# Two transformer blocks on one core: each engine's order made by a planner with other lengths and other priorities

## The reference

```python
mod = (_silu(L0_c) @ L0_wmod).reshape(L0_c.shape[0], 6, 1, -1)
sa, ca, ga, sb, cb, gb = (mod[:, 0], ..., mod[:, 5])
h = _layernorm(x) * (1 + ca) + sa
x = x + ga * _L0_attn_ref(h, ...)     # linear attention, 16 heads, features elu(q)+1 and elu(k)+1
h = _layernorm(x) * (1 + cb) + sb
x = x + gb * _L0_ffn_ref(h, ...)      # layernorm, 8 experts 128->512->128 with gelu, the two best per token
...                                   # mod of block 1
h = _layernorm(x) * (1 + ca) + sa
x = x + ga * _L1_attn_ref(h, ...)     # layernorm, softmax attention, 8 heads of 16, values of 128 summed over the heads
h = _layernorm(x) * (1 + cb) + sb
x = x + gb * _L1_ffn_ref(h, ...)      # h plus the best of 8 experts 128->128
```

## Time and profile before

| | before |
|---|---|
| median of 3 runs | 711.38 us |
| lowest and highest | 710.27 and 713.83 us |
| span of the profiled execution | 708.6 us |
| PE busy | 619.4 us (87%) |
| DVE busy | 511.1 us (72%) |
| ACT busy | 385.6 us (54%) |
| POOL busy | 334.4 us (47%) |
| matmuls of line 1507 (fill) | 165 |
| mean granted clock of TensorE | 0.951 |
| moved by DMA | 106.4 MB, mean 150 GB/s |

### The profile page before, as it was taken

How to read it: one execution, slowest core, us unless ns; L and a number is a source line. 1 busy time by engine, 2 the same in 40 slices (tenths; PEclk the granted TensorE clock), 3 DMA queues, 4 the chain that set the end, 5 groups by cost and what they waited for, 6 DMA issues and landing times. The chain is left out here.

```text
span 708.6 us, 12005 instructions
## 1 busy us (share of the span) xinstructions
PE 619.4 (87%) x3832; PEld 395.1 (56%) x3832; DVE 511.1 (72%) x1298; ACT 385.6 (54%) x861; POOL 334.4 (47%) x363
## 2 busy tenths in 40 slices
PE   8996887998899979979998799968798899789974
PEld 4665556997899779958654633212233344344332
DVE  5576959447458966155887389999888665958997
ACT  2342134678967557635699377737274456366410
POOL 5112287065478577767034153754214137106934
PEclk9998999999999989999999899979898899999998
DMA  8200325588678869999944615450501616421221
GB/s 339 91 1 1 107 103 179 174 280 286 212 258 274 284 216 332 296 295 302 291 151 104 163 45 105 119 107 28 89 1 45 134 52 128 125 91 53 53 59 30
DMA packets 47421, 106.40 MB, mean 150 GB/s; under 512 B 7440, under 2 KB 22608, under 8 KB 45824
## 3 DMA queue, kind: packets, MB, share of 16 engines
q1 hardware_dynamic: 41808, 94.82, 44.9%
q0 software_dynamic: 5120, 10.50, 5.1%
q10 hardware_dynamic: 432, 0.34, 0.2%
HBM read 80.26 MB, written 25.17 MB: 149 GB/s over the span
## 5 line engine op out<-in xcount | busy, mean ns | idle before, releaser
L1359 DVE TENSOR_REDUCE mxs<-PS 128x2 f32<-128x1024 f32 x128 | 152.2, 1221 | 60.0 <-PE PS L1687 59.5
L1027 ACT ACTIVATE bufa<-PS 128x512 f32<-128x512 f32 x256 | 134.8, 608 | 63.5 <-PE PS L1713 32.1
L986 ACT ACTIVATE bufb<-PS,bufb 128x128 f32<-128x128 f32 x368 | 103.6, 376 | 69.5 <-PE PS L1652 68.4
L1652 PE MATMUL PS<-bufb 128*128 128x128 f32 x736 | 101.2, 285 | 12.6 <-DMA bufb<-in_experts_dram 10.2
L1652 PEld LDWEIGHTS PS<-bufb 128*128 128x128 f32 x736 | 93.3, 199 | 20.7 <-issue 16.3
L1660 PE MATMUL PS<-bufb 128*128 128x128 f32 x736 | 101.2, 284 | 3.0 <-ACT bufb L986 3.0
L1660 PEld LDWEIGHTS PS<-bufb 128*128 128x128 f32 x736 | 93.8, 199 | 7.2 <-ACT bufb L986 4.1
L842 POOL DMA_INDIRECT slots_in<-bufb x64 | 65.1, 1017 | 63.8 <-DVE bufb L1305 45.4
L1703 PE MATMUL PS<-stk 108*128 108x512 bf16 x256 | 87.0, 400 | 6.5 <-ACT bufa L1027 3.6
L1687 PE MATMUL PS<-stk 96*128 96x512 bf16 x256 | 80.9, 408 | 8.2 <-DVE mxs L1359 6.2
L853 POOL DMA_INDIRECT bufb<-slots_out,bufb x64 | 62.1, 971 | 50.9 <-issue 43.8
(11 more groups left out here) (302 smaller groups left out, 1031.6 us busy)
## 6 DMA issues: line engine op xcount, KB each, us to landing
bufb<-in_experts_dram SPq DMA_DIRECT2D x92, 514.0 KB, 5.2
slots_out<-bufb SPq DMA_DIRECT2D x30, 256.0 KB, 4.5
stk<-split SPq DMA_DIRECT2D x56, 128.0 KB, 7.6
bufb<-slots_in SPq DMA_DIRECT2D x25, 256.0 KB, 3.3
split<-terms SPq DMA_DIRECT2D x8, 768.0 KB, 3.8
slots_in<-hb SPq DMA_DIRECT2D x2, 1536.0 KB, 9.0
stk<-split SPq DMA_DIRECT2D x8, 384.0 KB, 4.6
X<-in_x_dram SPq DMA_DIRECT2D x4, 512.0 KB, 6.5
```

Source lines behind the costliest of these rows:

```text
L986: last = nc.scalar.activation(hs[:, n % HR, fc, :], ps[:, P * fc:P * fc + P], ACT.Gelu_apprx_tanh, bias=ws[:, n % WR, F + fc:F + fc + 1])
L1027: nc.scalar.activation(probs[:, i % PR, j, :], psum("s2", i, j), ACT.Exp, scale=DH1 ** -0.5)\
L1359: nc.vector.tensor_reduce(mxs[:, gr % 2, 2 * j:2 * j + 2, h], psum("s1", i, j).rearrange("p (c n) -> p c n", c=2), axis=AX.X, op=ALU.max)\
L1652: last = nc.tensor.matmul(ps[:, P * fc:P * fc + P], ws[:, n % WR, P * fc:P * fc + P], xq[:, q % 2, P * x:P * x + P], start=True, stop=True)
```

## The change

The planner's tables and the rules of `arrange` are exchanged; the steps, what each emits, and the buffers stay. Every row of every engine's list is computed anew.

- `LENGTH` gives way to two tables: `BUSY`, how long a step holds its engine, and `SEEN`, after what time its result is seen by others.
- Lags of transfers come from `LANDS` (from the end of the issue to the landing) and `SERVED`: transfers of SP and POOL go through one queue in the plan, each for its time. `HOP` depends on the engine that waits.
- `URGENCY` by kind gives way to `PRIORITY` by engine, kind and pair (`part`), numbers between -2300 and 1981, often larger than the rank itself.
- `NEAR` is 0.2 instead of 0.
- A step that takes PSUM banks may only be placed when what the freeing step waits for has been placed.
- PE's steps take twice their time for `WARM` = 4.0 us after a planned wait of over `COOL` = 3.0 us; ACT's steps whose function stands in another table come 1.3 us later.

Lengths of landings are single numbers; no landing is planned late.

```diff
-LENGTH = {
-    ('PE', 'pc'): 1.84, ('DVE', 'pc'): 0.44, ('PE', 'pm'): 2.0, ('ACT', 'pm'): 1.01, ('PE', 'pr'): 1.0,
...
-LATENCY = {
-    ('SP', 'bxl', 'PE', 'bxt'): 4.5, ('SP', 'cst', 'PE', 's1'): 8.5,
-}
-HOP = 0.1
-URGENCY = {
-    'akx': -10, 'an2': 160, 'anm': 10, 'aq': 10, 'bn2': 80, 'btr': -10, 'byo': 80, 'ckp': 40, 'cn4': -80, 'cpt': 20,
...
-NEAR = 0
+BUSY = {
+    ('ACT', 'akv'): 1.57, ('ACT', 'aot'): 0.96, ('ACT', 'aq'): 2.06, ('ACT', 'atr'): 1.81, ('ACT', 'bgt'): 0.26, ('ACT', 'bh'): 1.02,
...
+LANDS = {
+    ('POOL', 'bga'): 2.8, ('POOL', 'bsc'): 2.9, ('POOL', 'rga'): 3.4, ('POOL', 'rsc'): 4.8, ('SP', 'bw'): 2.95,
+    ('SP', 'bxl'): 2.5, ('SP', 'byo'): 1.75, ('SP', 'ckp'): 4.0, ('SP', 'cst'): 7.3, ('SP', 'cto'): 3.35,
...
+SERVED = {
+    'bga': 1.0, 'bsc': 1.0, 'bw': 1.6, 'bxl': 0.85, 'byo': 0.85, 'ckp': 1.0, 'cst': 3.4, 'cto': 2.3,
...
+PRIORITY = {
+    ('ACT', 'akv'): (-1622, -426, -375, 1032), ('ACT', 'aot'): (-498, -755, 388, 1401), ('ACT', 'aq'): (-361, -581, 1256, -1203), ('ACT', 'atr'): (439, 1767, -40, 717),
...
+TABLE = {"blg": 1, "ex": 1, "aq": 1, "akv": 1, "bh": 2}
+TABLE_LOAD, COOL, WARM = 1.3, 3.0, 4.0
+NEAR = 0.2
...
     for k in reversed(line):
-        rank[k] = ops[k][0] + max([lag + rank[u] for u, lag in users[k]], default=0.0)
+        rank[k] = ops[k][0] + max([0.0] + [lag + rank[u] for u, lag in users[k]])
     for k in ops:
-        rank[k] += URGENCY.get(k[1], 0.0)
+        rank[k] += PRIORITY[k[:2]][part(k)]
...
-        clock[k[0]] = t + length
+        idle[k] = t - clock[e]
+        if e == "PE":
+            if idle[k] > COOL:
+                slow = t + WARM
+            if t < slow:
+                busy, seen = 2 * busy, seen + busy
+        elif e == "ACT":
+            table = TABLE.get(k[1], table)
+        clock[e], end = t + busy, t + seen
+        if SERVED.get(k[1]) and e in ("SP", "POOL"):
+            end = max(queue, end)
+            queue = end + SERVED[k[1]]
```

More of the change, by code:

```diff
@@ new lines @@
+SEEN = {
+    ('ACT', 'aot'): 1.07, ('ACT', 'atr'): 1.93, ('ACT', 'bh'): 1.14, ('ACT', 'btr'): 1.45, ('ACT', 'by'): 0.5, ('ACT', 'cpq'): 1.27,
+    ('ACT', 'ctr'): 1.45, ('ACT', 'dtr'): 1.07, ('ACT', 'ex'): 0.59, ('ACT', 'pm'): 1.01, ('ACT', 'pvo'): 0.58, ('DVE', 'an1'): 2.48,
+    ('DVE', 'an2'): 2.14, ('DVE', 'anm'): 1.72, ('DVE', 'apr'): 2.48, ('DVE', 'bcm'): 1.13, ('DVE', 'bgb'): 1.21, ('DVE', 'bgt'): 0.61,
+    ('DVE', 'blg'): 4.4, ('DVE', 'bn1'): 2.48, ('DVE', 'bn3'): 2.49, ('DVE', 'brk'): 4.14, ('DVE', 'cn1'): 1.64, ('DVE', 'cn3'): 1.64,
+    ('DVE', 'cn4'): 2.14, ('DVE', 'cpq'): 1.4, ('DVE', 'dl2'): 1.1, ('DVE', 'dn1'): 1.63, ('DVE', 'dw'): 2.92, ('DVE', 'dx'): 1.21,
+    ('DVE', 'dy'): 2.55, ('DVE', 'en1'): 1.69, ('DVE', 'fin'): 1.27, ('DVE', 'msp'): 0.79, ('DVE', 'mx'): 1.22, ('DVE', 'pvw'): 2.33,
+    ('DVE', 'rds'): 2.57, ('PE', 'akv'): 1.89, ('PE', 'akx'): 2.32, ('PE', 'anm'): 1.14, ('PE', 'aot'): 1.04, ('PE', 'apr'): 1.95,
[5 rows of a table added]
+}
@@ L329, in arrange @@
 def arrange(ops, start):
-    users, left, est, rank = {k: [] for k in ops}, {}, {}, {}
-    for k, (_, deps, _, _) in ops.items():
+    users, left, est, rank, giver = {k: [] for k in ops}, {}, {}, {}, {}
+    for k, (_, _, deps, _, give) in ops.items():
         left[k], est[k] = len(deps), 0.0
@@ L335, in arrange @@
             users[d].append((k, lag))
+        if give:
+            giver[("PE",) + give] = k
+    line, n = [], dict(left)
     todo = [k for k in ops if not left[k]]
-    line, n = [], dict(left)
     while todo:
@@ L361, in arrange @@
                 t = max(clock[e], est[k])
-                if ops[k][2]:
-                    t = max(t, min(vacant[ops[k][2]]))
+                if ops[k][3]:
+                    if any(d not in done for d in before_take[k]):
+                        continue
+                    t = max(t, min(vacant[ops[k][3]]))
+                if e == "ACT" and TABLE.get(k[1], table) != table:
+                    t += TABLE_LOAD
                 if t < 1e8:
@@ L366, in arrange @@
             if when:
-                k = min((k for k in when if when[k] <= min(when.values()) + NEAR), key=lambda k: (-rank[k], when[k]))
+                near = min(when.values()) + NEAR
+                k = min((k for k in when if when[k] <= near), key=lambda k: (-rank[k], when[k]))
                 if first is None or (when[k], -rank[k]) < first[:2]:
@@ L370, in arrange @@
         t, _, k = first
-        length, _, take, give = ops[k]
+        busy, seen, _, take, give = ops[k]
+        e = k[0]
         if take:
@@ L375, in arrange @@
             vacant[take][n], count[take][n] = 1e9, count[take][n] + 1
-        idle[k] = t - clock[k[0]]
-        clock[k[0]] = t + length
+        idle[k] = t - clock[e]
[10 more added lines that the diff above has]
+            queue = end + SERVED[k[1]]
         if give:
             cls, n, _ = use[give]
-            vacant[cls][n] = t + length
-        order[k[0]].append(k[1:])
-        ready[k[0]].remove(k)
+            vacant[cls][n] = end + HOP["PE"]
+        order[e].append(k[1:])
+        ready[e].remove(k)
+        done.add(k)
         for u, lag in users[k]:
-            est[u], left[u] = max(est[u], t + length + lag), left[u] - 1
+            est[u], left[u] = max(est[u], end + lag), left[u] - 1
             if not left[u]:
```

93 lines of the change are left out of this document (65 added, 28 removed), and 22 rows, old and new, of tables (BUSY, PRIORITY, SEEN).

## The result

The kernel after takes 716.0 us in the median of 20 runs (711.3 to 722.6), the kernel before on the same chip 712.6: a ratio of **1.006** with a 95% interval of 1.0035 to 1.0086. The forecast was 697 us. Runs more than 1.5% above the fastest of their kernel have no part in any ratio here, one of the kernel before at 2056 us among them. The change is slower by 0.6%, about the least that a measurement can tell, and 19 us above the forecast. The profiled execution spans 713.2 us; the sum that gave -14.0 us is judged against this: it is +4.6 us.

The account below looks back on a forecast made before the run. PE's order was taken to bound the kernel from 110 to 680 us, DVE's at the end. Terms summed to -14.0 us, so 694.6 + 2.8 gave 697 us, own range 686 to 706, 674 to 719 with rivals.

Parts of the forecast that it names:

- Opening: Up to the first experts: they start 6.4 us later, but earlier PE work and a vanished token wait give -4.0 us.
- Table loads: ACT switches between gelu and exp less often, 17 loads for 23, mostly in idle time: -2 us.
- Weights behind the stacks: Expert weights issued behind attention stacks: waits of 4 us (pair 2, tile 17) and 2.4 (pair 3, tile 9); -3 us.
- pair 3's experts: Pair 3's experts move behind the first attention, so score steps start after less PE work: -3 us.
- Gate of the stacks: Attention batches 4, 5 and 7: less PE work covers a stack's issue and landing, so PE waits more: +3 us.
- Last experts: Score steps now stand between the last experts' steps, so their 5.0 us of weight waits go: -5 us.
- End: From the last maxima on, DVE's list holds the same steps: nothing gained or lost.
- Collisions: Rival: three more DVE and POOL steps blocking each other cost 16 us and eat the gain, 711 to 713; chance 0.16.
- Late landings: Rival: stacks landing late at three short gates make PE wait and lower its clock, 719 us; chance 0.20.
- The plan holds: Rival: two fifths of PE's idle and low-clock time go rather than a sixth, 675 us; chance 0.19.
- three signs: Forecast wrong if first experts start after 119 us, attention's clock stays at 0.92 or falls, or a gate wait exceeds 5 us.
- the middle's -3: Between opening and last experts: weights behind the stacks -3, pair 3's experts -3, gate of the stacks +3 us.

Follow-up runs that it names:

- f3: Kernel after with the load of the stacks' fixed rows (ckp) and the turning of pair 3's tokens (btr) moved later; 0.9988 of before.
- f2: Kernel after with only pk, POOL's building of the stacks' constant patterns, moved later, ahead of the first gather; 1.0002 of before.
- e3: Kernel after with the end of the order of before, from a planned 595 us on; 0.9985 of before.
- g1: Kernel after with ckp, pair 3's btr and pk all moved later, plus the end of before; 0.9885 of before, 704.2 us.
- g4: Kernel before with only the opening of after, up to a planned 120 us; 0.9993 of before.
- f1: Order of before up to a planned 260 us, then that of after, then the end of before from a planned 610 us; 0.9928 of before.
- f4: Order of before to planned 540 us, that of after through the last experts, end of before from planned 625 us; 0.9933 of before.
- h1 to h4: Before and after with eight small transfers added ahead of each stack (before loses 18 us, after 35) or of eight expert weights (10 and 20 us).
- i1: g1 with eight small transfers ahead of each stack, run on another, slower chip; 0.9928 of before there.
- i2: g1 with eight small transfers ahead of eight expert weights, run on another, slower chip; 0.987 of before there.
- h2: Kernel after with eight small transfers issued ahead of each of the eight stacks; 1.0551 of before.

## Why the prediction was wrong

The forecast went through the steps that move most and priced each against its old surroundings. Three losses stand where it had no term or a zero: a transfer on SP that waits for DVE ahead of expert weights (ckp), a DVE step that came to stand beside a POOL step (ps beside pk), and the order of DVE's last steps ("nothing"). Each was taken away by runs of its own (f3, f2, e3: 14.6 us in sum), and all together they give back 12.5 us (g1). Of the gains that the forecast added up, one was found by itself, that of the last experts.

**Opening (forecast -4.0, found 0 by itself, +4.6 in after).** The first experts start at 121.47 us for 110.3, later than the 119 us that was named as the sign against: 11.2 us for 5.4 us more work, where 6.4 were forecast. The scatter starts at 87.51 us for 82.17 and the slots are turned at 117.83 (forecast 115); btr and blg then stand ahead of the first bh. By itself (g4) this costs nothing, as the wait behind it goes. Where the -4 went instead: the forecast had bn4 of pair 1 end before the first slots have landed, with no wait over 1 us at btr. Pair 1 has two roots on POOL, and only the first (bn1) came between the scatters, the second (bn3) stands behind them; bn4 starts at 112.41 us, as SP issues the load of the slots (112.28 us), takes 4.38 us for 2.14 beside POOL's sum, and PE waits 2.91 us at btr with the slots behind it (2.95 us in g4). No run moves that sum, so this part is argued from the rows. What made a loss of it in after is a step that the prediction doesn't have: ps of pair 1 comes to stand beside pk (f2). The part on DVE spoke of apr and an2 alone and didn't ask what POOL runs beside each moved step.

**Table loads (-2, not found).** The 17 loads came, but the term was sized by ACT's share of attention, and there are no loads there in before: 22 of its 23 stand between 110 and 410 us. f1 has 19 and f4 has 23, and they take the same time within 3 us. The term has no run of its own.

**No term for ckp (found about +5 of the time with btr, 12 in PE's lateness).** The prediction looked at SP's list where stacks stand in it, but not at the one other step that waits there. The rule was in its own words: what stands behind a waiting transfer waits with it. The waits named at tile 17 of pair 2 and tile 9 of pair 3 came in f1, at 4.63 and 2.40 us for 4 and 2.4; after itself has the second alone, 2.09 us at 411.02 us. "And no others" was wrong by 7.7 us.

**Weights behind the stacks and pair 3's experts (-3 and -3).** Together -4.4 in PE's lateness, but nothing in the time: f1 and f4 take the same within 3 us, so the full -6 isn't borne out, while -3 can't be told from nothing. Where it is spent stays open. After has waits for DVE behind this stretch, at cpv, cpq and mt (2.43, 2.70 and 3.19 us at 483, 527 and 555 us), but before has three of the same size (2.27, 3.27 and 2.62 us at 474, 512 and 540 us).

**Gate of the stacks (+3, found +0.7).** For batch 7 the last issue ends at 596.34 us, PE's first s1 stands at 604.96:

```profile
592.31 1.26 SPq L807 DMA_DIRECT2D stk<-split  x3
...
593.12 1.06 PE L1806 MATMUL PS<-bufa,vv 128*32 128x512 f32 x8 [0.46 <-ACT bufa L1120]
593.61 2.73 SPq L809 DMA_DIRECT2D stk<-split  x6
...
604.96 0.60 PE L1780 MATMUL PS<-stk 96*128 96x512 bf16 x2
```

That is 12.7 us behind the gate for 11.5 forecast, and PE is idle 3.4 us of it, as forecast, but in eight small waits for ACT and DVE, none of them for the stack. The work between was taken at full length without its own waits.

**Last experts (-5, found -6.4, f4 -5).** Right, mechanism and size: no wait for the last experts' weights is left in after or f4.

**End (0, found +6.4, e3 5 us).** "DVE's list from the last maxima on holds the same steps" was true and not the question. Two of them stand in another order, on the engine that is the bound there.

**The rivals.** *Collisions* were given 0.16 and three of them 16 us; one pair of places, ps beside pk, is 4 us (f2). Others stand at 520 us, where a normalising step takes 5.52 us and the same cast as in the earlier trace rows 2.20 us. They are no loss against before, which has its own (and the row of before behind these):

```profile
519.96 5.52 DVE L1231 TENSOR_SCALAR bufb<-X,mom,rstd 128x128 f32<-128x128 f32 x8
...
521.50 2.36 POOL L987 TENSOR_TENSOR X<-X,wa 128x1024 f32<-128x1024 f32 x1
...
526.67 3.78 PE L1768 MATMUL PS<-xTa,wqkv 128*128 128x512 f32 x4 [2.70 <-DVE mxs L1452]
...
528.24 2.20 DVE L1463 CAST mxt<-mxr 128x16 bf16<-128x16 f32 x1
```

```profile
533.51 4.81 DVE L1138 TENSOR_SCALAR bufb<-X,mom,rstd 128x128 f32<-128x128 f32 x8
```

*Late landings* had the right idea and the wrong place. Stacks landed 7.9 us behind their issue in the median, at most 10.0 (before 7.7 and 11.1), so none was late, and no wait of over 5 us stands at a gate; but h1 to h4 show that an added delay costs this order twice as much, and a DVE step that is late (ckp, btr) is such a delay. *The plan holds* had it the wrong way round. By the new planner's own lengths the order of before takes 679 us and that of after 649, 30 us less. Nothing of these 30 came. After's own POOL steps show one of the reasons: four indirect transfers are planned with 4.69 to 4.75 us, and successive scatter steps start every 5.0 to 5.3 us in the trace, as each transfer of 0.96 us is followed by 0.30 in which POOL waits for nothing that the profile shows.

Of the three signs that the forecast gave against itself one came, the first experts after 119 us; the granted clock in attention rose to 0.96, and no gate has a wait of over 5 us.

Of the sum of -14.0, -5 (last experts) came as forecast; the opening's -4, the table loads' -2 and the middle's -3 didn't show in any time; +5 (ckp and btr), +4 (ps beside pk) and +5 (the end) were missing. -5 + 14 is 9 where 4.6 were measured, or 3.4 in the medians, so some 5 us of gain would lie in the order that no run here has by itself. g1, -8 us against before (3 us either way), leaves 3 of them beside the last experts.

## What to carry to other kernels

When a planner moves everything, list for each in-order queue every step that waits for another engine, not only those that move most, and for each moved DVE step what GpSimd runs beside it. A plan that is shorter by its own lengths may have bought part of this with slack: put one equal delay into both orders and compare what each loses before believing the plan. A stretch-wise account (time less own work, at equal work) finds the places, but a single trace can't give their price; joining stretches of the two orders does, if the joint is where both have the same steps behind them.

## What the runs showed of the hardware

On one chip of those used the same kernel before takes 17% longer. In the trace of i1 from there a PE matmul has the length that it has elsewhere (0.275 us in the median), but ACT and DVE stand still for up to 11.6 and 10.0 us at a time, and PE then waits up to 9.2 us for them:

```profile
174.00 2.18 ACT L1218 ACTIVATE bufb<-PS,bufb 128x128 f32<-128x128 f32 x8 [11.56 <-remote]
...
175.20 0.90 PE L1877 MATMUL PS<-identf,bufb 128*128 128x128 f32 x3 [9.07 <-ACT bufb L1218]
```

"Remote" is what the view says where no recorded instruction of the core ended the wait. i1 and i2 have such waits of ACT and DVE, no other trace here has one. (i1 also has waits of 7.4 and 7.6 us for expert weights, but h2, with the same delay on another chip, has 8.3 and 9.1 us, so those tell nothing of the chip.) What that chip lacks isn't shown. A gain of 1% from an order is small beside it.
